# GNN layer with mixture of experts: self addition on TensorE, expert weights prepared during the edge gathers, low one-hots in halves, loads reordered

## What is computed

```python
xn = layernorm(x)
agg = jnp.zeros_like(xn).at[src].set(xn[dst])
x = x + concat(xn, agg) @ W.T + b
tokens = layernorm(x)
logits = tokens @ router_w.T ; top 2 of 8 experts, softmax weights combined
x = x + tokens + sum over the 2 experts of c[e] * (gelu(tokens @ w1[e] + b1[e]) @ w2[e] + b2[e])
```

## Time and profile before

| | us |
|---|---|
| median of three runs | 1116.87 |
| the profiled execution | 1117.8 |
| its span (first to last instruction) | 1116.1 |
| start of the edge stage's step 1 on TensorE | 61.54 |
| start of step 24 | 360.26 |
| first gather of agg_rows | 510.49 |
| TensorE busy over the span | 896.7 (80%) |
| VectorE busy over the span | 870.0 (78%) |
| ScalarE, GpSimd busy | 509.3 (46%), 455.6 (41%) |
| mean granted TensorE clock | 0.868 |

### The profile page before, as it was taken

The page is one execution under the profiler, slowest core; times in us unless marked ns, Lnnn a source line. Parts: engine busy times, 40 slices in busy tenths (PEclk is TensorE's granted clock), DMA queues, the critical chain, the costliest instruction groups (busy, mean ns, idle before and its releaser), DMA issues.

```text
span 1116.1 us, 28718 instructions
## 1 busy us (share of the span) xinstructions
PE 896.7 (80%) x9506; PEld 828.2 (74%) x9507; DVE 870.0 (78%) x1973; ACT 509.3 (46%) x1306; POOL 455.6 (41%) x527
## 2 busy tenths in 40 slices
PE   0156677777667799992999984699999999999997
PEld 0156667667666789991988972599999999999996
DVE  4769999899989677666787879477777777777776
ACT  0023333333322355551656543466666665666664
POOL 4000000000000477666777600366666766666664
PEclk9778888988989989996555556899999999999999
DMA  8931111111000255453666527122222222222230
GB/s 206 342 104 39 47 38 38 38 38 38 25 22 20 81 149 154 139 148 102 205 199 200 187 67 8 39 83 80 74 79 79 75 75 77 80 77 84 74 73 13
DMA packets 78968, 103.15 MB, mean 92 GB/s; under 512 B 22489, under 2 KB 64466, under 8 KB 78922
## 3 DMA queue, kind: packets, MB, share of 16 engines
q0 software_dynamic: 21408, 54.87, 17.5%
q1 hardware_dynamic: 57514, 47.73, 15.5%
HBM read 62.12 MB, written 44.02 MB: 95 GB/s over the span
## 4 chain that ended last, share of the span: by engine, by line
PE 56%; DVE 23%; issue 9%; SPq 5%; POOL 3%; ACT 2%; DMA 1%; DVEq 0%; POOLq 0%; ACTq 0%
PE bank L869 15%; PE bank L884 14%; PE bank L686 9%; DVE arena L976 8%; PE bank L701 6%; SPq L338 4%; DVE arena L964 4%; PE bank L835 3%; PE bank L879 2%; POOL arena L487 2%; PE bank L713 2%; PE bank L722 2%; PE bank L766 2%; DVE bst L1164 1%; ACT arena L622 1%
## 5 line engine op out<-in xcount | busy, mean ns | idle before, releaser
L475 POOL DMA_INDIRECT arena<-key_rows,cid x98 | 93.3, 952 | 395.3 <-DVEq L1085 358.9
L686 PE MATMUL bank<-arena 125*128 125x100 bf16 x1600 | 112.0, 251 | 141.7 <-DVE arena L976 120.2
L686 PEld LDWEIGHTS bank<-arena 125*128 125x128 bf16 x1600 | 107.8, 123 | 150.3 <-DVE arena L976 94.4
L884 PE MATMUL bank<-w2s,arena 128*128 x1500 | 197.8, 273 | 0.0
L869 PE MATMUL bank<-arena,w1s 128*128 128x128 f16 x3000 | 189.8, 220 | 6.9 <-issue 5.4
L869 PEld LDWEIGHTS bank<-arena,w1s 128*128 x3000 | 178.4, 98 | 14.0 <-issue 10.7
L502 POOL DMA_INDIRECT out<-arena,gidx x125 | 131.4, 1051 | 114.9 <-DVE arena L1293 99.9
L491 POOL DMA_INDIRECT arena<-tok_rows,gidx x125 | 121.9, 975 | 107.4 <-DVE gidx L1269 69.6
L884 PEld LDWEIGHTS bank<-w2s,arena 128*128 128x128 f16 x1500 | 146.8, 98 | 16.9
L701 PE MATMUL bank<-wgs,arena 128*128 128x256 f16 x1176 | 143.7, 275 | 0.0
L658 ACT ACTIVATE arena<-bank,b1s 128x128 f32<-128x128 f32 x500 | 142.0, 373 | 1.5 <-PE bank L869 1.5
(11 more groups left out here) (200 smaller groups left out, 1421.9 us busy)
## 6 DMA issues: line engine op xcount, KB each, us to landing
agg_rows<-arena SPq DMA_DIRECT2D x49, 256.0 KB, 2.2
tok_rows<-arena SPq DMA_DIRECT2D x14, 896.0 KB, 4.6
big<-x SPq DMA_DIRECT2D x6, 1792.0 KB, 16.9
arena<-w SPq DMA_DIRECT2D x16, 256.0 KB, 2.8
arena<-tok_rows,gidx POOLq DMA_INDIRECT x125, 2.8
out<-arena,gidx POOLq DMA_INDIRECT x125, 2.5
big<-x SPq DMA_DIRECT2D x1, 1664.0 KB
arena<-key_rows,cid POOLq DMA_INDIRECT x98
```

The source lines that it names most:

```text
L475: gp.indirect_dma_start(er[:, b % 2, s, :], None, key_rows, bass.IndirectOffsetOnAxis(cid[:, t:t + 1], 0)).then_inc(er_full[b % 2], 16)
L686: last = mm(bank[4][:, h * TP:(h + 1) * TP], oh_lo[:, at, :, c % 2], oh_hi[:, at, :, c % 2], start=(c == 0), stop=(c == GC - 1))
L884: last = mm(to, a[:, u % 4, at:at + P], parts[x, w, c], start=False, stop=(n == 5))
```

## The change

- **Self addition.** In edge steps, TensorE begins each half of bank 2 or 3 with a float32 product of x by `idents`, an identity times SCALE (64), and adds the linear layer on top. ScalarE copies the sum back to x with scale 1/64 (`take_self`), and TensorE waits for `self_taken` instead of `self_added`. This holds for pairs 0 to 22; from pair 23 on VectorE adds as before.
- **Expert weights.** High parts go to ScalarE's pairs d = 25 to 40, low parts to VectorE's node steps 26 to 41, loads 2 to 15 to SyncE's stores 24 to 37. The loops over node pairs are written out on TensorE, ScalarE and SyncE.
- **Halves.** `low_onehots` is two instructions of 4096 elements; `onehots_used` is incremented after 32 products and after 64. The first half stands ahead of `take_groups`, the second behind it.
- **Loads.** SyncE waits for the source indices before it issues anything else; then bias, x chunk 0, W, router, b1, edge rows, x chunk 1; then the bias rows; then x chunks 2 to 6 and the tail; then the key rows.

```diff
         @block.sync
+            sp.wait_ge(s_src, 16)
             sp.dma_start(bgs[:, :], bg.rearrange("(a d) -> a d", a=1).broadcast_to([P, D])).then_inc(s_small, 16)
+            load_x(0)
+            sp.dma_start(wgf, wg).then_inc(s_wg, 16)
...
+            load_x(1)
             sp.wait_ge(s_small, 48)
             sp.dma_start(agg_rows[NP:NP + P, :], bgs[:, :]).then_inc(s_brow, 16)
             sp.wait_ge(brow_zeroed, 1)
             sp.wait_ge(bparts_ready, 1)
             for n in range(3):
                 sp.dma_start(brow[n:n + 1, :], bpart[:, n, :]).then_inc(s_brows, 16)
+            for c in range(2, len(s_x)):
+                load_x(c)
...
             def store_and_load(i, k, w, e):
                 store_agg(i, k)
-                sp.wait_ge(w_prep, i)
-                load_weight(w, e, 1 - k)
+                sp.wait_ge(w_prep, i - IB)
+                load_weight(w, e, k)
...
+            def take_self(i, k):
+                sc.activation(xs[:, ds(2 * i, 2), :].rearrange("p a d -> p (a d)"), bank[2 + k][:, :], ACT.Copy,
+                              scale=1.0 / SCALE).then_inc(self_taken, 1)
             def act_pair(d, k, groups=True, ws=None, e=None):
...
                     take_products(i, k, known and i < 2)
+                if groups and (not known or i >= 0):
+                    take_self(i, k)
                 if not known or 0 <= i + 1 < T // 2:
                     take_low(i + 1, 1 - k, known and i + 1 < 2)
                 if ws is not None:
-                    high_weight(i, k, ws, e)
+                    high_weight(d - ND, 1 - k, ws, e)
...
         @block.tensor
                 for h in range(2):
                     for c in range(GC):
...
-                last.then_inc(onehots_used, 1)
+                    last.then_inc(onehots_used, 1)
...
+                    if early:
+                        mm(bank[2 + k][:, h * D:(h + 1) * D], idents[:, :],
+                           xs[:, ds(2 * i + h, 1), :].rearrange("p a d -> p (a d)"), start=True, stop=False)
...
         @block.vector
             def edge_step(d, k, base):
                 high_products()
...
                 layer_norm(d, k)
-                if not known or d >= LAG + 1:
-                    add_self(d - LAG - 1, 1 - k)
-                if ws is not None:
-                    low_weight(d - LAG - 1, 1 - k, ws, e)
...
-                dve.wait_ge(onehots_used, d + 1)
+                else:
+                    dve.wait_ge(onehots_used, 2 * d + 1)
+                    low_onehots(d + 1, 0)
+                dve.wait_ge(onehots_used, 2 * d + 2)
                 take_groups(d)
                 if not known or d < ND - 1:
-                    low_onehots(d + 1)
+                    low_onehots(d + 1, 1)
...
             def node_step(d):
...
-                add_self(d - LAG - 1, (d - LAG - 1) % 2)
+                if d - LAG - 1 >= IB:
+                    add_self(d - LAG - 1, (d - LAG - 1) % 2)
+                m = d - ND - 1
+                if 0 <= m < 2 * E:
+                    low_weight(m, m % 2, (w1s, w2s)[m // E], m % E)
                 if d < T // 2:
                     layer_norm(d, d % 2)
```

More of the change, by code:

```diff
@@ L371, in _ @@
                 load_weight(w1, k, k)
[L372 to L384, removed]
+            with sp.Fori(0, (IB - 1) // 2) as j:
                 for k in range(2):
                     store_agg(2 * j + k, k)
-            store_agg(T // 2 - 1, 0)
+            for i in range(IB - 1, IB + 1):
+                store_agg(i, i % 2)
+            for i in range(IB + 1, IB + 2 * E - 1):
+                m = i - IB + 1
+                store_and_load(i, i % 2, (w1, w2)[m // E], m % E)
+            for i in range(IB + 2 * E - 1, T // 2):
+                store_agg(i, i % 2)
             sp.wait_ge(w_prep, 2 * E)
@@ L576, in act_pair @@
                 if ws is not None:
-                    high_weight(i, k, ws, e)
+                    high_weight(d - ND, 1 - k, ws, e)
             deviation(0, 0)
             act.wait_ge(s_brows, 48)
[L581 to L592, removed]
+            for d in range(4):
+                act_pair(d, d % 2)
+            with act.Fori(2, ND // 2) as j:
                 for k in range(2):
@@ L595, in _ @@
             act_pair(ND - 1, (ND - 1) % 2)
[L596 to L600, removed]
+            for m in range(E):
+                act_pair(ND + m, (ND + m) % 2, groups=False, ws=w1s, e=m)
+            act.wait_ge(s_keys, 64)
+            for m in range(E, 2 * E):
+                act_pair(ND + m, (ND + m) % 2, groups=False, ws=w2s, e=m - E)
+            for d in range(ND + 2 * E, T // 2 + LAG):
                 act_pair(d, d % 2, groups=False)
@@ L702, in node_linear @@
                                           wgs[:, w, c, half * D:(half + 1) * D],
-                                          start=(half == 0 and n == 0), stop=(n == 5))
+                                          start=(not early and half == 0 and n == 0), stop=(n == 5))
                             n += 1
@@ L746, in _ @@
             pe_pair(ND - 1, (ND - 1) % 2)
-            pe_pair(ND, ND % 2, groups=False)
-            with pe.Fori((ND + 1) // 2, T // 4 + 1) as j:
-                for k in range(2):
-                    pe_pair(2 * j + k, k, groups=False)
-            pe_pair(T // 2 + 1, 0, groups=False)
+            for d in range(ND, T // 2 + LAG):
+                pe_pair(d, d % 2, groups=False)
             pe.wait_ge(consts3_ready, 11)
@@ L1040, in _ @@
             for d in range(4):
-                edge_step(d, d % 2, did.base + did.n, **({"ws": w1s, "e": 0} if d == LAG + 1 else {}))
-            for c in range(1, len(s_x)):
-                dve.wait_ge(s_x[c], 16 if c < len(s_x) - 1 else 32)
-            before = did.base + did.n - 4 * per
-            def edge_steps(first, last, ws=None, less=0):
-                with dve.Fori(first // 2, last // 2) as j:
-                    for k in range(2):
-                        d = 2 * j + k
-                        edge_step(d, k, before + per * d, ws=ws, e=None if ws is None else d - LAG - 1 - less)
-            edge_steps(4, E + 2, w1s)
-            edge_step(E + 2, 0, before + per * (E + 2), ws=w1s, e=E - 1)
-            edge_step(E + 3, 1, before + per * (E + 3), ws=w2s, e=0)
-            edge_steps(E + 4, 2 * E + 2, w2s, E)
-            edge_step(2 * E + 2, 0, before + per * (2 * E + 2), ws=w2s, e=E - 1)
-            edge_step(2 * E + 3, 1, before + per * (2 * E + 3))
-            edge_steps(2 * E + 4, ND - 1)
-            edge_step(ND - 1, (ND - 1) % 2, before + per * (ND - 1))
+                edge_step(d, d % 2, did.base + did.n)
+            for c in range(1, 2 * (ND + 1) // x_chunk + 1):
+                dve.wait_ge(s_x[c], 16)
+            before = did.base + did.n - 4 * per
+            with dve.Fori(2, ND // 2) as j:
+                for k in range(2):
+                    edge_step(2 * j + k, k, before + per * (2 * j + k))
+            edge_step(ND - 1, (ND - 1) % 2, before + per * (ND - 1))
+            for c in range(len(s_x)):
+                dve.wait_ge(s_x[c], 16 if c < len(s_x) - 1 else 32)
             def node_step(d):
```

49 lines of the change are left out of this document (30 added, 19 removed).

## The result

The changed kernel takes **1056.1 us** (median of four runs, 1055.66 to 1057.52) against 1117.2 for the kernel before beside it: ratio 0.946 (95% interval 0.944 to 0.9475). The profiled execution took 1055.74, its span is 1053.3, 62.8 us shorter than before.

What follows compares the result with a forecast made beforehand. A loop between TensorE and VectorE was taken to bound the edge steps, TensorE the node stage. Gains 43.2 + 16.7 - 5.0 = 54.9 took 1117.8 to 1062.9, with the median 0.9 lower: 1062.0 us, range 1054 to 1069.

Steps and rivals of the forecast that it cites:

- likeliest case: Whole kernel: the forecast of 1062.0 us, given chance 0.63, with its own range 1054 to 1069.
- Edge stage: Edge steps: VectorE's unbroken row binds at 11.0 us a step (bounds 10.8 to 11.4), gaining 43.2 us.
- TensorE's step: Edge steps: TensorE's work, with two added float32 products, takes 10.6 us against 11.0, leaving 0.4 to spare.
- The signs I had named: Edge steps: among them, TensorE idle under 1 us and at a clock above 0.95.
- The rival that TensorE binds: Edge steps: 64 products take 5.53, a step 11.7, 16 us less gained, total 1078; chance 0.15.
- The identities: Edge steps: two added float32 identity products on TensorE for the self addition, taken as 1.0 us a step.
- Start: Before step 1: indices land at 10.5, step 1 starts at 44.85 instead of 61.54, gaining 16.7 us (bounds 10 to 22).
- The bias rows: Start: landed by 40.3, early by 4.5 us for step 1.
- Node stage: Node pairs: weights make TensorE's input late by 0.6 us per two-pair block; 5.0 us lost (bounds 0 to 12).
- The weight loads: Node stage: they land in 2.8 us, with about 5 us until their high part; nothing counted.
- The rest: After 510.49 us nothing is changed: 0 us.
- Slower: Edge stage: TensorE's clock stays at its lower level (granted 0.5), step 17.7 us, total 1216; chance 0.02.

Runs made afterwards that it cites:

- experiment 4: Changed kernel with the self addition back on VectorE in every pair; 1070.51 us, ratio 0.9585.
- experiment 5: Changed kernel with the expert weights back in edge steps 2 to 18; 1063.53 us, ratio 0.953.
- experiment 3: Changed kernel with the low one-hots again as one instruction behind the taking; 1094.26 us, ratio 0.980.
- experiment 9: experiment 3 plus 16 never-read products per edge step on TensorE behind the dense part; ratio 0.981, on a chip where the kernel before took 1312.0 us.
- experiment 7: Changed kernel with the source indices loaded in two parts, 112 and 13 partitions; 1055.58 us, ratio 0.945.
- experiment 1: Changed kernel with the old order of loads and no wait for the source indices; 1071.86 us, ratio 0.959.
- experiment 2: Kernel before with the new order of loads alone; 1097.87 us, ratio 0.983.
- experiment 6: Kernel before with halved low one-hots alone; 1091.39 us, ratio 0.977.
- experiment 8: Changed kernel without SyncE's wait for the source indices, new order of loads kept; 1060.39 us, ratio 0.949.
- experiment 12: Changed kernel with split index load, GpSimd's iota made before the identities, and 12 never-read products per edge step on TensorE; 1053.51 us, ratio 0.942.
- experiment 11: Changed kernel with the weighting of the small high one-hots moved to GpSimd; ratio 0.973, on a chip where the kernel before took 1312.0 us.

## Why the prediction was right

The forecast was 1062.0; 1056.1 came. The likeliest case happened in the edge stage, the start and the rest. The node stage came out with the other sign, and it makes up 5.7 of the 7.9 us that the span gained beyond the sum; the start makes up 1.1, the edge stage 0.9, the rest 0.2.

- **Edge stage, 43.2 predicted, 44.1 measured.** VectorE's unbroken row bounds the step: 10.78 worked out, 11.0 forecast, 10.95 measured; a half takes 2.28, and 2.21 from its start to the next one's (2.20 taken, bounds 2.17 and 2.32). Experiments 4 and 5 confirm it, since 0.69 and 0.75 us put back on VectorE lengthen the step by 0.67 and 0.75. That work off VectorE pays mainly together with the halves is shown by experiment 3: 0.27 a step without them, 0.94 with (12.01 to 11.07).
- **TensorE's step, the term that was mis-sized.** I had 10.6 us, of which 4.43 for the group products, and 0.4 us to spare. The 64 products take 3.10; the step is 8.9 with 2.1 idle. I took the products' time as fixed, though the trace of before showed 4.43 and 5.53 for the same instructions, and 3.09 at 205.73. It goes with the granted clock (1.00, 0.65 and 0.50), and low clocks get rarer as the idle time before the products shrinks: mostly 3.3 to 4.2 us before (18 of 22 groups slow), 2.05 to 2.13 now (4 of 22), 1.00 in experiment 9 (none). The idle time alone doesn't decide it, since one and the same gives slow and fast groups; what else does is open. The signs I had named were TensorE idle under 1 us and a clock above 0.95; they came as 2.1 us and 0.95. The rival that TensorE binds (0.15) was further off than I said: in experiment 4, with half of the groups slow, VectorE's row still sets the step. The identities were 0.86, not 1.0.
- **Start, 16.7 predicted, 17.8 measured.** The indices landed at 9.08 instead of 10.5: the rate over 5 us was 133 GB/s, more than the 83 that I had read from a half microsecond at its beginning. Of these 1.4 us, 1.1 had reached the products of step 1 (43.77 for 44.85). The DMA share, 0.32, stayed what it had been (0.29). That is the k rule of the Trainium skill (DMA: Bandwidth & Descriptors, Why a DMA increments its semaphore by 16 and not by 1): 125 partitions are served by 5 engines, since 5 is their largest divisor up to 16, and 5 of 16 is 0.31. The row agrees, and so does experiment 7, where 112 and 13 partitions reach 1.02. The figure of the bandwidth table, against which I weighed the row, didn't bear on this load. The bias rows were early by 8.0 us (35.74 against 43.77), not 4.5; experiments 1 and 2 put the loads at 15.8 and 19.1.
- **Node stage, 5.0 lost predicted, 0.7 gained measured.** The mechanism was there (low part ahead of the norm, TensorE's input late), but the size was off. Two pairs take 9.93 to 9.99 while weights are prepared, against 9.68 without them, 0.3 instead of the 0.6 per block: in my chain the norm ended 9.1 us after the first pair's transposes and the normalised input was there after 10.4; in the trace the norm ends after 8.8 (390.91 + 0.16 - 382.29) and the input is there after 9.9 (391.10 + 1.09). I had added up whole lengths of VectorE's instructions, whose starts lie a little before the recorded end of the one ahead (390.01 against 389.44 + 0.66 = 390.10), and a gap of 0.2 that is 0.03 in the trace. The writing out of the loops gave back 1.4, which the diff showed and I had costed at nothing without a row. The halves gave 3.3 in experiment 6, between step 24 and the first gather, where I had counted nothing for the last step. Experiment 5 shows that the weights do cost 3.8 there and 4.4 in all, near my 5.0; what I had missed was mostly on the side of gain. The 0.7 itself is partly luck: the seven kernels with the same node stage (the changed one and experiments 1, 3, 4, 7, 8 and 12) take 149.5 to 151.5 for this stretch, and the changed kernel is the shortest. The weight loads landed in 4.1 us, not in 2.8, still within the 5 that I had allowed.
- **The rest**, 605.4 against 605.6: nothing, as said.
- **Slower.** The clock did not stay at its lower level: granted 0.95 in the edge stage with the float32 products in it.

## What to carry to other kernels

When a loop goes round two engines, cut the piece that both wait for in two before taking work off either: experiment 3 lacks only that cut and loses 38 us. The same products can take half as long again after a gap (4.64 against 3.10), so in a loop that waits for TensorE a shortened gap pays twice; before pricing TensorE's groups, read the granted clock over them, and ask what idle time will stand before them. And an engine moved earlier meets the work that used to be over by then: look at what the other engine does in the new place.

## What the runs showed of the hardware

- **TensorE's speed after a gap.** In all fourteen traces the groups of steps 3 to 24 that take over 4 us are exactly those in which the granted clock falls to its lower level. Of the groups with under 1.4 us of TensorE's idle time before them none was slow (89 groups), with 2.0 to 2.2 us 34 of 87, with over 2.6 us 75 of 94. So a gap makes a slow group likelier and does not settle it.
- **GpSimd beside VectorE.** GpSimd's selects of 0.28 took 1.03 to 1.07 beside VectorE's int32 instructions in experiment 12, and VectorE's 1.07 became 2.61 beside an iota. In the start of the changed kernel GpSimd needs 11.39 us for 14 selects that took 5.11 before. The Trainium skill (SBUF — State Buffer, Who interferes with whom) says that the two share a port pair, and that for some instructions whoever issues first holds it for the whole instruction. The traces agree: 2.61 is 1.07 and nearly the iota's 1.52, and in experiment 11 VectorE's 0.44 instead of 0.16 ends with GpSimd's instruction (193.30 and 193.28).
- **Partition counts.** 125 partitions load at 133 GB/s and 112 + 13 at 365, with one line of code more.
- **The same kernel took 17% longer on one chip** (1312 against 1117), with an edge stage that ran at its usual pace. Whole times are to be compared only between kernels that ran beside each other.
